# A selective scan and attention kernel: on TensorE, jobs between next input and sums, and the jobs of the main steps dealt to other units

## The reference, cut to what matters

```python
xz = einsum('bsd,ed->bse', rmsnorm(h), ip_w);  xi, z = split(xz, 2)      # 512 + 512 channels
xi = silu(conv4(xi) + cb);  dt, Bm, Cm = split(einsum('bse,fe->bsf', xi, xp_w))
dt = softplus(dt @ dtp_w.T + dtp_b);  dA = exp(dt * A);  dBu = dt * Bm * xi   # 16 states a channel
h_t = dA_t * h_(t-1) + dBu_t;  y_t = sum over states of h_t * C_t             # the scan over time
out = ((y + xi * D) * silu(z)) @ op_w.T;  h = h + out
```

## Time and profile before

| what | us |
|---|---|
| median of 3 runs (7791.1 to 7796.77) | 7791.65 |
| the profiled execution, its own time | 7799.68 |
| its span, first to last instruction | 7797.9 |
| one middle step, scan 0 to the next step's scan 0 | 89.77 |

### The profile page before, as it was taken

The page is one execution under the profiler, slowest core; times in us unless marked ns, Lnnn a source line. Parts: engine busy times, 40 slices in busy tenths (PEclk is TensorE's granted clock), DMA queues, the critical chain, the costliest instruction groups (busy, mean ns, idle before and its releaser), DMA issues. The chain is left out here.

```text
span 7797.9 us, 204883 instructions
## 1 busy us (share of the span) xinstructions
PE 7253.6 (93%) x86656; PEld 5168.7 (66%) x86656; DVE 6486.4 (83%) x6490; ACT 5772.7 (74%) x10871; POOL 5816.9 (75%) x2981
## 2 busy tenths in 40 slices
PE   7998799999988999999988999999989999999989
PEld 4666577777764677777764677777764677777765
DVE  5999799999984699999973699999973799999972
ACT  5777788888864688888864788888854788888853
POOL 4994599899970599999970598899960689899960
PEclk9999999999999999999999999999999999999999
DMA  3323222223210222222210222222210222222210
GB/s 104 90 82 94 69 75 70 75 75 97 76 47 23 82 75 70 78 86 89 70 52 21 78 75 70 87 88 77 71 52 22 78 75 74 97 80 73 70 52 11
DMA packets 736041, 552.24 MB, mean 71 GB/s; under 512 B 355844, under 2 KB 679364, under 8 KB 698008
## 3 DMA queue, kind: packets, MB, share of 16 engines
q1 hardware_dynamic: 735128, 539.13, 22.2%
HBM read 519.25 MB, written 19.79 MB: 69 GB/s over the span
## 5 line engine op out<-in xcount | busy, mean ns | idle before, releaser
L1229 DVE TENSOR_TENSOR_SCAN arena<-arena,ps 128x512 f32<-128x512 f32 x4608 | 5291.7, 1202 | 389.8 <-issue 254.1
L1454 POOL TENSOR_TENSOR arena<-arena 128x1024 f32<-128x1024 f32 x2240 | 5248.0, 2367 | 489.7 <-DVE arena L1229 461.3
L904 ACT ACTIVATE arena<-arena,rate 128x511 f32<-128x511 f32 (+1 forms) x4608 | 3033.5, 709 | 11.6 <-DVE arena L1229 11.2
L569 PEld LDWEIGHTS ps<-arena 64*128 64x128 f32 x36864 | 2322.4, 189 | 1073.1 <-issue 614.8
L569 PE MATMUL ps<-arena 64*128 64x128 f32 x36864 | 2712.8, 285 | 184.1 <-DVE arena L1229 175.3
L588 PE MATMUL ps<-csts,arena 64*128 64x64 f32 x35840 | 1519.3, 223 | 8.3 <-POOL arena L1454 8.0
L588 PEld LDWEIGHTS ps<-csts,arena 64*128 64x128 f32 x35840 | 1436.3, 139 | 18.4 <-POOL arena L1454 12.3
L627 PE MATMUL ps<-arena 128*128 128x512 f32 x1152 | 594.5, 632 | 164.6 <-DVE arena L1259 154.3
L1474 POOL TENSOR_TENSOR arena<-arena 128x512 f32<-128x512 f32 x288 | 371.2, 1289 | 410.6 <-PE ps L654 242.5
L668 PE MATMUL ps<-arena 128*128 128x512 f32 x1120 | 588.6, 631 | 3.1 <-DVE hT L1269 3.1
L632 PE MATMUL ps<-arena 128*128 128x512 f32 x1120 | 567.0, 621 | 3.7 <-DVE arena L1259 2.3
(11 more groups left out here) (116 smaller groups left out, 6454.1 us busy)
## 6 DMA issues: line engine op xcount, KB each, us to landing
arena<-c_rows SPq DMA_DIRECT2D x288, 1024.0 KB, 5.2
arena<-b_image SPq DMA_DIRECT2D x576, 256.0 KB, 3.2
arena<-ip_x SPq DMA_DIRECT2D x20, 512.0 KB, 4.4
arena<-ip_z SPq DMA_DIRECT2D x20, 512.0 KB, 4.5
arena<-op_w SPq DMA_DIRECT2D x20, 512.0 KB, 6.7
hT<-xT SPq DMA_DIRECT2D x16, 512.0 KB, 3.8
arena<-w SPq DMA_DIRECT2D x8, 1024.0 KB, 5.2
out<-arena SPq DMA_DIRECT2D x64, 128.0 KB, 1.7
```

The lines of the kernel that those rows point to most:

```text
L569: i = nc.tensor.matmul(o, dtxT[half[h], c, b, :], diagB[half[h], pair, b, :].rearrange("p (i s) -> p i s", s=Q), start=True, stop=True)
L904: nc.scalar.activation(o, i, ACT.Exp, scale=rate[:, ph.layer(n), g:g + 1]).then_inc(decay.sem, 1)
L1229: nc.vector.tensor_tensor_scan(hs[:, place(n, v) + g % 2, :], dA[:, g % RING, :], pair[:, g % Q::Q], 1.0 if ph.main() else 0.0, ALU.mult, ...
L1454: nc.gpsimd.tensor_tensor(hs[:, a:a + 2, :], hs[:, a:a + 2, :], Crep[:, 2 * pair:2 * pair + 2, :], ALU.mult).then_inc(prod.sem, 1)
```

## The change

On PE the order within a unit becomes input, jobs, sum, in every unit and in the prefix too. The tables of the main steps are dealt anew: z1 moves from units 31 and 0 to unit 0, z2 and z3 to units 2 and 3, ms to 13, out0.2 to 16; on ACT `yev1` and `yev2` move from units 19 and 26 to 21 and 27, `carry` from 14 to 16, dxT0 behind xi1, the skips earlier; on DVE gates, norms and a residual by one to two scans; on POOL `squares` from 4 to 9, `carry` from 16 to 14, dtx1 and dtx2 by one unit. No computation is added or removed.

```diff
-MAIN_BANK = {"z0": 0, "z1": 1, "z2": 0, "z3": 1, "yt2": 0, "yt3": 1, "xp": 0, "dxT3": 1, "bT": 1, "ms": 1, "dt0": 0,
+MAIN_BANK = {"z0": 0, "z1": 0, "z2": 0, "z3": 1, "yt2": 1, "yt3": 1, "xp": 0, "dxT3": 1, "bT": 0, "ms": 1, "dt0": 0,
...
-MAIN_PE = {0: [("z1.1", 1), ("z2.0", 1)], 2: [("z3.0", 1), ("z2.1", 1)], 3: [("z3.1", 1)], 5: [("yt2", -1)],
-           6: [("xp.0", 1), ("xp.1", 1), ("yt3", -1)], 7: [("xp.2", 1), ("xp.3", 1)], 8: [("dxT3", 0)], 9: [("bT", 1)],
-           10: [("dt2", 1), ("dt3", 1)], 12: [("dt0", 1), ("dt1", 1)], 14: [("ms", 2)],
-           15: [("out0.0", -1), ("out0.1", -1), ("out0.2", -1)], 16: [("out0.3", -1)], 18: [("xi0.0", 2)],
-           19: [("xi0.1", 2), ("yt0", 0)], 20: [("dxT0", 1)], 21: [("xi1.0", 2), ("xi1.1", 2)], 22: [("yt1", 0)],
-           24: [("xi2.0", 2), ("xi2.1", 2)], 25: [("dxT1", 1)], 26: [("out1.0", -1)],
+MAIN_PE = {0: [("z1.0", 1), ("z1.1", 1)], 2: [("z2.0", 1)], 3: [("z3.0", 1), ("z2.1", 1), ("z3.1", 1)],
+           5: [("yt2", -1)], 6: [("xp.0", 1), ("xp.1", 1), ("yt3", -1)], 7: [("xp.2", 1), ("xp.3", 1)],
+           8: [("dxT3", 0)], 9: [("bT", 1)], 10: [("dt2", 1), ("dt3", 1)], 12: [("dt0", 1), ("dt1", 1)],
+           13: [("ms", 2)], 15: [("out0.0", -1), ("out0.1", -1)], 16: [("out0.2", -1), ("out0.3", -1)],
+           18: [("xi0.0", 2)], 19: [("xi0.1", 2), ("yt0", 0)], 20: [("dxT0", 1)], 21: [("xi1.0", 2), ("xi1.1", 2)],
+           22: [("yt1", 0)], 24: [("xi2.0", 2), ("xi2.1", 2)], 25: [("dxT1", 1)], 26: [("out1.0", -1)],
...
-           30: [("dxT2", 1), ("z0.0", 2), ("z0.1", 2)], 31: [("z1.0", 2)]}
-MAIN_ACT_FIRST = {3: [("yev3", -1)], 12: [("yev0", 0)], 19: [("yev1", 0)], 26: [("yev2", 0)]}
-MAIN_ACT = {1: [("z1", 1)], 2: [("silu_x", 1), ("silu_z", 0)], 3: [("z3", 1), ("z2", 1), ("sq", 2)], 8: [("xp", 1)],
-            9: [("dxT3", 0), ("bT", 1)], 10: [("skip2", 0)], 11: [("dt2", 1), ("dt3", 1)],
-            12: [("dt0", 1), ("dt1", 1), ("skip3", 0)], 13: [("rstd", 2)], 14: [("soft", 1), ("carry", 1)],
-            19: [("xi0", 2)], 20: [("dxT0", 1)], 21: [("xi1", 2)], 22: [("skip0", 1)], 24: [("skip1", 1)],
-            25: [("xi2", 2), ("dxT1", 1)], 27: [("xi3", 2)], 30: [("dxT2", 1)], 31: [("z0", 2)]}
-MAIN_DVE = {11: [("gate2", -1)], 16: [("gate3", -1)], 32: [("norm0", 2)], 33: [("norm1", 2)], 37: [("res0", -1)],
-            40: [("gate0", 0)], 41: [("tap00", 2)], 42: [("tap01", 2), ("tap02", 2)], 46: [("tap10", 2)],
-            47: [("tap11", 2)], 48: [("tap12", 2)], 49: [("gate1", 0)], 52: [("tap20", 2)],
+           30: [("dxT2", 1), ("z0.0", 2), ("z0.1", 2)]}
+MAIN_ACT_FIRST = {3: [("yev3", -1)], 12: [("yev0", 0)], 21: [("yev1", 0)], 27: [("yev2", 0)]}
+MAIN_ACT = {1: [("z1", 1)], 2: [("silu_x", 1), ("silu_z", 0)], 3: [("z3", 1), ("sq", 2), ("z2", 1)], 8: [("xp", 1)],
+            9: [("dxT3", 0), ("skip2", 0), ("bT", 1)], 11: [("dt3", 1), ("skip3", 0), ("dt2", 1)],
+            12: [("dt0", 1), ("dt1", 1)], 13: [("rstd", 2)], 14: [("soft", 1)], 16: [("carry", 1)],
+            20: [("xi0", 2), ("skip0", 1)], 21: [("xi1", 2), ("dxT0", 1)], 22: [("skip1", 1)],
+            25: [("xi2", 2), ("dxT1", 1)], 27: [("xi3", 2)], 29: [("dxT2", 1)], 31: [("z0", 2)]}
+MAIN_DVE = {12: [("gate2", -1)], 17: [("gate3", -1)], 30: [("norm0", 2)], 34: [("norm1", 2)], 35: [("res0", -1)],
+            40: [("gate0", 0)], 41: [("tap00", 2), ("tap01", 2)], 42: [("tap02", 2)], 46: [("tap10", 2)],
+            47: [("tap11", 2)], 48: [("tap12", 2)], 50: [("gate1", 0)], 52: [("tap20", 2)],
...
-MAIN_POOL = {3: [("dtx3", 0)], 4: [("squares", 2)], 16: [("dtx0", 1), ("carry", 1)], 18: [("dtx1", 1)],
-             27: [("dtx2", 1)]}
+MAIN_POOL = {3: [("dtx3", 0)], 9: [("squares", 2)], 14: [("carry", 1)], 16: [("dtx0", 1)], 19: [("dtx1", 1)],
+             26: [("dtx2", 1)]}
...
                     adds = to is not None and ph.gated(to) and (scans(ph, n) or n == ph.steps)
-                    if adds and w % CU:
-                        sum_pair(ph, to, w)
                     for name in last_events(LAST_PE, ph, n, v):
                         job(ph, ph.steps - 1, name)
                     for m, name in events("pe_at", ph, n, v):
                         job(ph, m, name)
                     if ph.main() and n == ph.steps:
                         begun_attention(ph, v)
-                    if adds and w % CU == 0:
+                    if adds:
                         sum_pair(ph, to, w)
```

## The result

The changed kernel takes 7894.84 us in the median of four runs (7893.11 to 7898.88), the kernel before 7792.89 beside it: a ratio of 1.013, 95% interval 1.0116 to 1.0144. It is slower, as forecast, but by 102 us where 41 were forecast, and outside the range. The profiled execution took 7893.11 us; beside the 7799.68 of before, its span is 93.4 us longer.

A forecast was written before the change was run, and what follows sets the result against it. PE's work and waits bound each step: work -0.9, waits +1.6, so +0.7 us. 52 middle steps (36), four first steps (2.4) and six prefix steps (2.4) give +41: 7791.65 + 41 = 7832 us, range 7768 to 7868.

The forecast's parts named there:

- What bounds the kernel: Middle steps, 89.77 us each: PE's work of 86.53 at full clock plus its waits of 3.3 set the time.
- the walk: Hand simulation of one middle step, every engine's list in order; gave 89.7 before the change, trusted to about half a microsecond.
- PE's work: Middle step: order saves 0.6, new deal of z saves 0.3, so -0.9 us.
- its waits: PE's waits in a middle step: 4.9 us against 3.3 before, +1.6.
- The bounds of the passages: PE's switches between 64-row and 128-row products: 0.10 per unit either way, -2.2 to +1 us a step around -0.6.
- The cover of POOL's `carry`: POOL unit 14: `carry` waits some 5 us for ACT's, but products are 2.3 us early for sum 15; cost nothing.
- rival "much slower": ACT's `carry` 2 us later than walked, products 15 to 17 miss their sums: +0.8 more a step, 7875 us; chance 0.08.
- The prefix: Six prefix steps, new order with old tables: between -1 and +1, taken as +0.4 us each, 2.4 in all.
- rival "faster": Input before a job and sum behind it cost nothing more: -0.5 us a step, 7764 us; chance 0.18.
- rival "no change": `yev1` and xi3 each 0.6 earlier than walked, two waits halve: step 89.4 to 89.9, 7782 to 7802 us; chance 0.22.
- the waits at 0.9 and 1.2: PE's waits at sum 16 for `yev1` (unit 20) and at dxT2 (unit 30), forecast at 0.85 and 1.3 us.
- the last two steps of a block about zero: Last two steps of each block: no change in time, as no jobs run two steps ahead; bounds 2 each way.

The follow-up runs named there:

- runs with old ends: Changed kernel with old tables in opening steps and last two bodies, yt2 there on bank 0: 7862.63 us; with the old order too: 7728.76 us.
- ms and xi0 put back: Changed kernel, but in the opening steps ms, squares, and ACT's copies of xi0 and dxT0 return to their old units: 7879.2 us.

## Why the prediction was wrong in size

*What bounds the kernel, and the walk* held. The middle step was forecast at 90.5 and is 90.43. That it comes so near is in part luck, as within it two small errors cancel: PE's work fell by 0.36, not 0.9 (86.17, above the 85.6 to 86 that was to be seen), and its waits are 4.3, not 4.9. The runs tell the parts of the work: 86.04 with the new deal in the old order against 86.53 before, so the deal saves 0.5, and the order adds 0.1 where I had it save 0.6. With the old tables the order adds 0.45 (86.98 at full clock). The bounds of the passages (-2.2 to +1) held. The prediction reads them wrongly, though: around its -0.6 they are -1.6 to +1.6 a step and not -1.3 to +1.6, and 52 times that is 83 us either way, 7749 to 7915, more than "a little further" than 7768 to 7868. The measured time lies within these bounds, but not for that reason.

*The cover of POOL's `carry`* held: the wait of 5.0 shows, and no product misses its sum. The rival "much slower" by that stall did not happen. The prefix cost +2.2, forecast +2.4; that is luck too, since the same prefix took 876.0, 880.9 and 882.5 us in three kernels.

*The rival "faster"* needed sums behind jobs that cost nothing more. In the changed kernel's page the weight loads of sums stood idle for 791.7 us, 640.3 of it issue (group L588 above: time in which they waited for nothing that the profile shows); before it was 18.4, and the inputs' loads (L569) had 1073.1, now 174.6. The two lines of the page before:

```profile
L569 PEld LDWEIGHTS ps<-arena 64*128 64x128 f32 x36864 | 2322.4, 189 | 1073.1 <-issue 614.8
...
L588 PEld LDWEIGHTS ps<-csts,arena 64*128 64x128 f32 x35840 | 1436.3, 139 | 18.4 <-POOL arena L1454 12.3
```

The idle time by issue went with the place, from the inputs' loads (614.8) to the sums' (640.3): it is in front of whichever product of 64 rows stands behind a job. What decides the rival is PE's work: it needed 1.2 less a step, and with the new tables the order adds 0.1. The rule of the Trainium skill that the prediction weighed ("TensorE: Matmul & The Clock Gate", Part 2, step by step) is that weight loads are pulled ahead of running matmuls when their row groups don't conflict or when they go to the background weight buffer. The prediction left these conditions out; loads that ran ahead do not show at these passages, and the trace doesn't tell which buffer a load goes to. *The rival "no change"* fails with the waits at 0.9 and 1.2, not half.

*The step that failed* is the term "the last two steps of a block about zero (no jobs two steps ahead), bounds 2 each way", and that the openings had no term at all. Two facts were in the listing and not used. The openings run by unit number between MLP products: a job that moves by one unit there can move by a whole product. And the bank edit, harmless in a middle step, meets fq0 in step 15. For step 14 the zero held (-0.3 in the sum of four). Measured, the openings cost +30.5 us, step 15 +21, the attention +3. Of the 30.5, the old tables in the opening steps alone bring back 25, of which ACT's two copies hold about 12 and ms about 5. Of the 21, 14 are yt2's bank, shown by the run that moves it alone; between other kernels with and without that edit the difference is 8 to 20. The rest is mostly that step 15 of the last block took 116.2 in the profiled execution of before, at a clock of 0.98, where its three others took 121.0 to 122.1 at 0.90 to 0.91. With the ends, 41 + 54 = 95 against 93.4 in the profiles; the medians differ by 102, since the profiled execution of before lies 6.8 above its median and that of the changed kernel 1.7 below its own.

What stays open is how much of the ends a repair returns in the total. The runs with old ends show the waits gone, and parts that they leave alone longer at a lower clock; one execution of each can't tell what of that is the edit's and what is the spread. Nor can I say from these records why one block's attention takes 140.8 and the next, of the same program, 144.7.

## What to carry to other kernels

When jobs in hand-written lists are dealt anew, look for every place where the same lists run between other work (a prologue, the next block's opening, a tail): there a unit has another length, and a bank another neighbour. In an in-order queue, ask of each piece of work that is moved behind another whether it was filling a wait: this order cost 1.2 us a step by one sum of 0.7 us. And test the parts of a compound change apart: here one half was worth -1.5 us a step and the other +2.1, or +5.1 on the old tables. Where an edit's gain does not reach the total, compare first the stretches that the edit can't touch.

## What the runs showed of the hardware

The price of an idle PE can be more than the idle time. Behind a wait of 4.58 us, PE's granted clock was 0.59 for the next 7.3 us (block 1, 4282.2 to 4289.5), and two matmuls took 2.04 for 1.10; behind a wait of 2.86 in the kernel before it was 1.00. But the length of the wait alone does not decide it. The two matmuls of ms follow a wait of 4.57 to 4.58 in seven kernels, and took 1.77 to 2.05 at all 21 places (three in a kernel); they follow one of 2.86 in seven others, and took 1.10 in 9 and 1.84 to 2.05 in 12. One of the 12, with ms and xi0 put back (L625 is ms there), and the busy time by stretch behind it, at a granted clock of 0.62:

```profile
4283.89 1.92 PE L625 MATMUL ps<-arena,csts 128*128 128x512 f32 x2 [2.86 <-POOL arena L1472]
```

```profile
4283.89:4288.40 4.51, 4.51 (x6) 1.60 (x6) 1.32 (x2) 2.49 (x4) 0.00 (x0) 0.62 0.00 0
```

What sets them apart was not tried. Equal work in equal order then takes different times: step 15 of the changed kernel, four blocks:

```profile
2221.09:2323.83 102.74, 84.61 (x1100) 62.13 (x1098) 84.27 (x83) 62.36 (x124) 81.47 (x36) 0.88 0.14 48
3990.92:4087.41 96.49, 77.63 (x1108) 58.88 (x1108) 83.92 (x82) 62.27 (x124) 82.53 (x36) 0.96 0.16 51
5757.08:5856.60 99.52, 81.37 (x1100) 60.98 (x1098) 84.17 (x83) 62.20 (x124) 81.51 (x36) 0.91 0.14 48
7525.47:7626.64 101.17, 83.07 (x1100) 61.49 (x1098) 84.15 (x83) 62.31 (x124) 81.45 (x36) 0.90 0.14 47
```

From its first to its last scan it takes 96.5 to 102.7 us, in the order of the clock, 0.96 to 0.88. A gain of a few us in one such stretch can't be read from one total.
